# Narrower selections, one add per chunk and a longer message ring in a graph network kernel

## The reference

```
weight = einsum('rb,bio->rio', comp_l, bases_l)      # 8 matrices of 128x128
h = einsum('ni,rio->nro', x, weight)
msg = h[src, etype]                                  # one row of 128 per edge
agg = segment_sum(msg * norm[:, None], dst)          # norm: 1 / edges of that destination and type
x = agg + x @ root_l + bias_l                        # then batch norm and relu, but for the last layer
```

## Time and profile before

| | us |
|---|---|
| median of 3 runs | 5364.16 |
| lowest and highest run | 5345.99 and 5364.67 |
| profiled execution, its own time | 5356.81 |
| its span | 5354.7 |
| PE, DVE, POOL, ACT busy | 3940.1, 3231.6, 2710.8, 1109.8 |
| L936 (visit product) on PE, 4980 passes | 1904.9 |
| L604 (gather) on POOL, 2490 instructions | 2530.2 |
| L1615 (selections) on DVE, 2490 instructions | 884.4 |
| L1645 (adds) on DVE, 1245 instructions | 522.3 |

### The profile page before, as it was taken

One profiled execution on the slowest core, in us unless ns is written; L12 is line 12 of the kernel. 1 busy time (PEld: TensorE's weight loads), 2 busy tenths in 40 slices (PEclk: granted clock), 3 DMA queues, 4 the chain that ended last, 5 costly groups with the idle time before them and its releaser, 6 DMA issues.

```text
span 5354.7 us, 66549 instructions
## 1 busy us (share of the span) xinstructions
PE 3940.1 (74%) x14160; PEld 1992.2 (37%) x14160; DVE 3231.6 (60%) x8826; ACT 1109.8 (21%) x1906; POOL 2710.8 (51%) x2646
## 2 busy tenths in 40 slices
PE   7017676777767777777777867777777669999997
PEld 3013343333333333343333333333333334444443
DVE  6965455444445666666666466666666676455464
ACT  4000000000013333333333433333333340000000
POOL 0666677676652666666666066666666610000000
PEclk9556666656668888989888988898888979999998
DMA  6011111111125444444444534444444438888895
GB/s 230 6 35 45 47 46 46 46 47 46 46 68 192 123 120 122 125 122 125 121 123 125 218 110 124 123 124 124 124 122 122 124 95 300 297 288 296 291 300 164
DMA packets 416155, 716.49 MB, mean 134 GB/s; under 512 B 98515, under 2 KB 322056, under 8 KB 415535
## 3 DMA queue, kind: packets, MB, share of 16 engines
q1 hardware_dynamic: 331562, 544.93, 30.1%
q0 software_dynamic: 84096, 166.09, 12.3%
q10 hardware_dynamic: 130, 1.20, 0.1%
HBM read 431.85 MB, written 279.93 MB: 133 GB/s over the span
## 4 chain that ended last, share of the span: by engine, by line
PE 58%; issue 16%; POOL 8%; DVE 7%; another core or an unknown queue 6%; DMA 3%; ACT 1%; SPq 1%; DVEq 0%; POOLq 0%; ACTq 0%
PE psum L936 20%; PE psum L923 11%; PE psum L984 7%; PE psum L985 7%; PE psum L912 6%; POOL area L604 6%; PE psum L883 3%; POOL key_list L574 3%; DMA area<-msg_table,visit_src 2%; PE psum L898 1%; DVE agg_and L1645 1%; DVE edge_area L1163 1%; DVE area L1615 1%; PE psum L999 1%
## 5 line engine op out<-in xcount | busy, mean ns | idle before, releaser
L604 POOL DMA_INDIRECT area<-msg_table,visit_src x2490 | 2530.2, 1016 | 1419.0 <-issue 600.7
L936 PE MATMUL psum<-area 128*128 128x256 f32 x4980 | 1904.9, 483 | 341.0 <-DMA area<-msg_table,visit_src 127.3
L936 PEld LDWEIGHTS psum<-area 128*128 128x128 f32 x4980 | 1023.8, 234 | 861.3 <-issue 566.9
L1645 DVE TENSOR_TENSOR agg_and<-agg_and,psum 128x256 f32 x1245 | 522.3, 420 | 1204.9 <-PE psum L936 539.8
L654 ACT CAST bufE<-psum 128x512 f16<-128x512 f32 x1507 | 883.3, 586 | 1666.5 <-PE psum L923 796.6
L923 PE MATMUL psum<-bufE,carry 128*128 128x512 f16 x1506 | 634.3, 421 | 677.4 <-issue 503.4
L1615 DVE TENSOR_SCALAR area<-iota,agg_and 128x256 f32<-128x256 f32 x2490 | 884.4, 417 | 14.2 <-ACT agg_and L670 12.6
L984 PE MATMUL psum<-area,edge_area 128*128 128x512 f16 (+1 forms) x1911 | 691.1, 369 | 16.2 <-DMA area<-counts 9.0
L985 PE MATMUL psum<-area,edge_area 128*128 128x512 f16 (+1 forms) x1911 | 690.6, 369 | 0.0
L923 PEld LDWEIGHTS psum<-bufE,carry 128*128 x1506 | 148.0, 98 | 1324.6 <-issue 1308.9
L912 PE MATMUL psum<-bufE 128*128 128x512 f16 x1507 | 627.1, 416 | 2.0 <-remote 0.7
(11 more groups left out here) (326 smaller groups left out, 1904.2 us busy)
## 6 DMA issues: line engine op xcount, KB each, us to landing
area<-counts SPq DMA_DIRECT2D x252, 896.0 KB, 4.5
counts<-bufE SPq DMA_DIRECT2D x1507, 128.0 KB
msg_table<-area SPq DMA_DIRECT2D x147, 512.0 KB, 2.6
area<-msg_table,visit_src POOLq DMA_INDIRECT x2490
agg_and<-counts SPq DMA_DIRECT2D x162, 128.0 KB, 4.5
area<-counts SPq DMA_DIRECT2D x21, 224.0 KB, 3.3
bufE<-inv_sqrt SPq DMA_DIRECT2D x2, 1568.0 KB, 11.3
out<-cur SPq DMA_DIRECT2D x12, 256.0 KB
```

The source lines that it names most:

```text
L604: g.indirect_dma_start(out=msg[:, n % MV, :], out_offset=None, in_=msg_table, in_offset=bass.IndirectOffsetOnAxis(ap=visit_src[:, v:v + 1] ...
L936: t.matmul(psum[:, banks[c % len(banks)], at:at + W2], msg[:, n % MV, :], visit_sel[:, n % SV, :], start=v % 2 == 0, stop=v % 2 == 1).then ...
L1645: v.tensor_tensor(to, to, psum[:, banks[c % len(banks)], at:at + W2], ALU.add).then_inc(visit_added, 1)
```

## The change

The selection of a visit becomes 128 columns wide, counted from the visit's own block, and is no longer counted from the pair's. PE puts the product into the chunk's bank at a column that a register gives (a distance of the visit's block from the block of the chunk's first visit, up to three blocks), so several visits may add up in the same columns. A product of zeros over all 512 columns opens the bank. DVE adds the 512 columns of a chunk at once. `visit_pack` now holds, for two chunks, the first block and the three distances; DVE loads it as before, PE loads eight of its words per 16 chunks. `keep_visits` loses the seven instructions that shifted the columns; `plan_visits` computes the new packing (five small instructions in place of three). The selections take half their room, and the message ring takes the freed room: MV = 32.

```
-MV = 16
+MV = 32
-W2 = 256
+PACKS = 8
-        agg_and = sb("agg_and", [128, COLS + 128])
+        agg_and = sb("agg_and", [128, COLS + BW - 128])
-        msg = area[:, 4096:4096 + MV * D].rearrange("p (b d) -> p b d", d=D)
+        msg = area[:, SV * 128:SV * 128 + MV * D].rearrange("p (b d) -> p b d", d=D)
-        visit_sel = staging.rearrange("p (s n) -> p s n", n=W2)
+        visit_sel = staging[:, 0:SV * 128].rearrange("p (s n) -> p s n", n=128)
...
+        def shifted(pack, by):
+            return (pack << -by) if by < 0 else (pack >> by)
+        def chunk_column(pack, c):
+            return shifted(pack, 12 * (c % 2) - 7) & (COLS - 128)
+        def visit_column(pack, c, j):
+            return shifted(pack, 12 * (c % 2) + 6 + 2 * (j - 1) - 7) & (BW - 128)
...
+                def columns_of(c):
+                    if c % (2 * PACKS) == 0:
+                        first = c // 2
+                        packs[0] = nc.values_load_multi_w_load_instructions(
+                            visit_pack[0:1, first:min(first + PACKS, NVW)], engines=(mybir.EngineType.PE,))[1]
+                    pack = packs[0][c // 2 % PACKS]
+                    return [0] + [visit_column(pack, c, j) for j in range(1, len(chunk_of(c)))]
...
                 def sums(c):
                     blocks = list(built(k, c))
+                    columns = columns_of(c)
+                    bank = banks[c % len(banks)]
                     if c >= len(banks):
-                        pe.wait_ge(visit_added, pairs(k, pairs_of(c - len(banks))[-1] + 1))
-                    for v in chunk_of(c):
+                        pe.wait_ge(visit_added, chunks(k, c - len(banks) + 1))
+                    t.matmul(psum[:, bank, :], zeros16[:, 0:128], zeros16[:, :], start=True, stop=False, skip_group_check=True)
+                    for j, v in enumerate(chunk_of(c)):
                         n = visits(k, v)
-                        at = v % CH // 2 * W2
+                        to = psum[:, bank, bass.ds(columns[j], 128)] if j else psum[:, bank, 0:128]
+                        if j:
+                            pe.compute_val(columns[j] * 4)
                         pe.wait_ge(visit_ready, n + 1)
                         pe.wait_ge(visit_in[n % MV], visit_loads(k, v))
-                        t.matmul(psum[:, banks[c % len(banks)], at:at + W2], msg[:, n % MV, :], visit_sel[:, n % SV, :],
-                                 start=v % 2 == 0, stop=v % 2 == 1).then_inc(visit_summed, 1)
+                        t.matmul(to, msg[:, n % MV, :], visit_sel[:, n % SV, :], start=False, stop=v == chunk_of(c)[-1],
+                                 skip_group_check=True).then_inc(visit_summed, 1)
...
             def keep_visits():
-                step, other = block_step, elsewhere
-                block_of = visit_dst.rearrange("p (q j) -> p q j", j=2)
-                link(v.memset(step, 0.0))
-                link(v.tensor_tensor(step.rearrange("p (q j) -> p q j", j=2)[:, :, 1], block_of[:, :, 1], block_of[:, :, 0], ALU.subtract))
                 dve.wait_ge(tiles_turned, 1)
...
-                link(v.scalar_tensor_tensor(out=step, in0=step, scalar=128.0, in1=visit_dst, op0=ALU.mult, op1=ALU.add))
-                link(v.tensor_scalar(other, visit_dst, 128.0, NODST, ALU.is_ge, ALU.mult))
-                link(v.tensor_tensor(step, step, other, ALU.add))
-                link(v.tensor_scalar(other, visit_dst, 0.0, NODST, ALU.is_lt, ALU.mult))
-                link(v.tensor_tensor(visit_dst, step, other, ALU.add))
...
-                        v.tensor_scalar(to, iota[:, 0:W2], low, norm[:, at:at + 1], ALU.is_equal, ALU.mult).then_inc(visit_ready, 1)
+                        v.tensor_scalar(to, iota[:, 0:128], low, norm[:, at:at + 1], ALU.is_equal, ALU.mult).then_inc(visit_ready, 1)
...
-                    for q in pairs_of(c):
-                        column, at = pair_column(pack, q), q % 2 * W2
-                        if pairs(k, q):
-                            dve.wait_ge(visit_added, pairs(k, q))
-                        to = agg_and[:, bass.ds(column, W2)]
-                        v.tensor_tensor(to, to, psum[:, banks[c % len(banks)], at:at + W2], ALU.add).then_inc(visit_added, 1)
+                    if chunks(k, c):
+                        dve.wait_ge(visit_added, chunks(k, c))
+                    to = agg_and[:, bass.ds(chunk_column(pack, c), BW)]
+                    v.tensor_tensor(to, to, psum[:, banks[c % len(banks)], :], ALU.add).then_inc(visit_added, 1)
```

31 lines of the change are left out of this document (14 added, 17 removed).

## The result

| | before | changed |
|---|---|---|
| median, same chip (us) | 5360.8 (4 runs) | 5414.19 (4 runs) |
| span of the profiled execution | 5354.7 | 5408.4 |
| mean granted clock | 0.826 | 0.804 |

The change makes the kernel slower: ratio 1.0100, 95% interval 1.0083 to 1.0116. The forecast was 5270 us.

The account below looks back on a forecast made before the run. POOL's gathers and waits were taken to bound layer 0, the count blocks' chain layers 1 and 2. 5356.8 - 100 - 8 - 6 + 20 = 5263, plus 7 for the runs' scale: 5270 us; own range 5220 to 5330, with rivals 5080 to 5390.

Parts of the forecast that it names:

- Ring of 32: Layer 0: with 32 message slots POOL's 100 us of waits for PE's counter go, -100 us; nothing in layers 1 and 2.
- second rival: Layer 0: POOL runs 16 further, then waits twice as long, half as often; the 100 us stay, 5370 us; chance 0.16.
- Registers in layer 0: PE in layer 0: a visit has 1.31 us for some 0.8 us of PE work, so the added instructions cost nothing.
- Registers in layers 1 and 2: PE at a chunk's start: first registers, zero product and loads exceed the idle time before L923, +60 us per layer.
- Product: Layers 1 and 2: the narrower visit product shortens links at half clock and visits without a block, -50 us per layer.
- net of +10 per layer: Layers 1 and 2: registers at +60 and the narrower product at -50 leave +10 us in each layer.
- Selections: Layer 0: DVE's selections of 128 columns disturb POOL's gathers less, -8 us, with ends 0 and -46.
- keep_visits: Path to the first gather: the instructions removed there save 6 us.
- Adds: DVE, all layers: one add per chunk saves DVE 0.4 us, but DVE waits for PE, so 0.
- Late releases shrink: Layers 1 and 2: narrower products or selections cut ACT's 259 us of remote waits, sign below 150; 5080 us; chance 0.2.
- The registers lengthen the chain: L923's link at a chunk's start, layers 1 and 2: registers exposed from 0.51 us per chunk make it slower, 5420 us; chance 0.14.

Follow-up runs that it names:

- run 16: Not a run or kernel: words of "POOL does run 16 further", meaning POOL's gathers get 16 visits further ahead; no time or ratio belongs to it.
- a_gate: The changed kernel, with DVE writing one element between its wait for a chunk's products and the add's register instructions; ratio to the kernel before 1.0103.
- a_noreg: The changed kernel with every visit at column 0 of its bank, without the added register instructions and loads on PE; 5387.26 us, ratio to the kernel before 0.9972.
- b_again: The kernel before, unchanged, profiled again on the chip of the second set; 5407 us.
- r_sp0_3: The changed kernel with 16 message slots and layer 0's messages by plain transfers from SP instead of POOL's gathers, met late counters; layer 0 took 479 us.
- b_dose: The kernel before with some 2000 more register instructions on PE over the three layers and 13 loads per layer; ratio to the kernel before 1.0006.
- a_ring16: The changed kernel with the message ring back at 16 slots; ratio to the kernel before 1.0086, layer 0 at 1223 us.
- b_fill: The kernel before with a product of zeros between each block's count and its carry in layers 1 and 2; ratio to the kernel before 1.0001.

## Why the prediction was wrong

Its sum for layer 0 was -108 us (ring -100, selections -8), and the changed kernel has +20 there and +10 behind it. That is 138 of the 144 us by which 5414 misses 5270.

- *Ring of 32, -100: failed, and first.* The changed kernel has POOL's waits of 154 us where 141 were. The step counted "23 at most, under 32": POOL one to seven gathers ahead of PE, and a counter at most 16 behind. The 16 holds (32 less 17 to 26 is 6 to 15 at the end of the waits), the one to seven doesn't. It was POOL's lead under a ring of 16, and with 32 slots the lead grew to 17 to 26. The step lifted one of three limits of 16 visits. The counter stayed late, and DVE waits for the same counter with a ring of 16 selections, of which PE then had at most 10 before it. That layer 0 doesn't shorten with either ring alone is measured; that the other limits are what keeps it long is read from these counts, and what makes the counter late stays open beyond its place, POOL's gathers. The second rival ("the ring only postpones", chance 0.16) has the outcome right, a layer 0 that keeps its 100 us, and the mechanism in part: POOL does run 16 further, but the waits are not twice as long and half as often (59 gaps where 61 were).
- *Registers in layer 0, "hidden": a smaller error.* 1.31 us per visit were to cover 0.8 us of work, by a price of 36 ns per instruction. That row was taken in a prompt moment. 385 instructions of 0.70 us and more make 272 us in spells, where visits are then up to 4.9 us apart. Yet most of it lay under waits that the late counter brings anyway: without registers layer 0 takes 1209 us, in a_gate 1221. So the registers cost some 12 us there, and don't explain why the ring gained nothing.
- *Registers in layers 1 and 2, +60:* 28 and 25 us (a_gate against a_noreg, on two chips on which the kernel before took 5407 us). *Product, -50:* a_noreg against b_again, which hold the narrower product and the zero product, differ by -18 and +2; the granted clock fell from 0.88 to 0.86 and 0.84, and whether that took the gain back is not shown. The net of +10 per layer was measured as +3 and +29: near in layer 1, by two errors that cancel, and 19 us short in layer 2.
- *Selections, -8:* in layer 0 the gather's mean went from 1.003 to 0.998 us, 4 us in all, and in prompt runs from 0.992 to 0.994, nothing; in each of layers 1 and 2 it is 21 us there. The price was near the other end, and in other layers. With late counters the gather is shorter there too (1.024 to 0.996 us in layer 2), and the layers are not. The rule cited from the Trainium skill (SBUF - State Buffer, Who interferes with whom) fits layer 0; in layers 1 and 2, where other instructions of DVE lie between, the rows don't agree with a zero.
- *keep_visits, -6:* right, -8. *Adds, 0:* right as far as the rows show, L1652 takes 0.683 us.
- *Late releases shrink (0.2):* its sign came (118.6 us, under 150) and its gain did not. The sign was no proof, since the same time stood under another name.
- *The registers lengthen the chain (0.14), 5420 us:* right in sign and in what brings the loss, the register instructions. That its 5420 lies beside the 5414 is luck: it added 170 us in layers 1 and 2 to gains of 114 elsewhere, and the runs have 32 us in these layers and no gain of 114. Its place was too narrow (a chunk's head in layers 1 and 2), and its price came from a count at 0.1 us and not from 0.70.

With prompt counters the ratio of 0.9889 would be 5301 us on the first chip's scale, within the forecast's 5220 to 5330. That is luck too: there the ring gives nothing, the registers cost nothing, and the gain is 41 us of shorter gathers in layers 1 and 2 and 7 us of keep_visits.

What the prediction could have seen: both late releases that it quotes lie under POOL's gathers, shows DVE held by the same counter as POOL, and PE's own queue had 24 instructions near 0.70 us in layer 2. At that rate, 24 of 4682, the 2033 added ones would still have been priced at some 7 us a layer. That the rate would rise to 221 of 6715 no row showed.

## What to carry to other kernels

Bound the price of an added sequencer instruction by its slowest rows in the same stage, not by its median, and find out what stands behind each one: in front of an instruction that waits, it has cover. Before deepening a ring, list every other limit on the same counter, and ask how far the producer will then run ahead; its lead under the short ring says nothing of that. When a counter seems late, look for what is under way at that time. And run the kernel before beside each set: one and the same kernel took 5407 and 4910 us on one chip, and the verdict on the change turned from +1.0% to -1.1% with it.

## What was not expected of the hardware

- While POOL's indirect gathers are issued, in one condition of the chip, semaphore updates of PE and of DVE come late (DVE its own by 4.78 us, PE's by up to 27 us), and register instructions of PE take 0.70 us in place of 0.036. With plain transfers of as many bytes from SP in the same layer neither was seen (r_sp0_3).
- The slow instructions grow faster than the instructions: in layer 0 of the first set, on one chip, none of 829 in a_noreg (ring of 32), 49 of 1489 in b_dose and 231 of 2860 in a_ring16.
- The condition costs the kernel before 0.5 ms: 5407 against 4910 us on the same chip, layers of 1214, 1263 and 1281 us (b_again) against 1078, 1092 and 1104 (b_fill, which is the kernel before but for products of zeros that cost nothing).
- The granted clock of layers 1 and 2 follows it: 0.88 in the kernel before with late counters, 0.98 or more in its variants with prompt ones. What the lower clock itself costs was not separated.
- The gathers set the floor of layer 0: 830 x (0.99 + 0.30) us, gather and gap, are 1071 of its 1078 us with prompt counters; with plain transfers the layer takes 477.
- Neither kernel is best in both conditions. Whether a version with the narrower selections and no registers on PE can be both is open; a_noreg, which leaves the placement out, has 0.9972 with late counters and 0.9889 with prompt ones.
